# Two decoder layers on one core: the order of part three set anew, with the turning steps and value products as streams of their own, and GpSimd's divisions in halves

## The reference

```
x = ln(x + attn(x))          # causal, 16 heads of 64, bias on q, k, v
x = ln(x + xattn(x, ctx))    # 16 heads of 64, 64 keys, no mask
x = ln(x + ffn(x))           # an attention over nested widths 128, 64, 32, 16: 8 heads of 16
```

## Time and profile before

| | |
|---|---|
| median of three runs | 1757.98 us |
| the profiled execution | 1755.88 us, of which the span from first to last instruction is 1753.8 us |
| PE busy | 1543.1 us (88%), 14032 instructions |
| DVE busy | 1148.2 us (65%) |
| ACT busy | 958.4 us (55%) |
| POOL busy | 485.2 us (28%) |
| mean granted TensorE clock | 0.968 |

### The profile page before, as it was taken

The page is one execution under the profiler, slowest core; times in us unless marked ns, Lnnn a source line. Parts: engine busy times, 40 slices in busy tenths (PEclk is TensorE's granted clock), DMA queues, the critical chain, the costliest instruction groups (busy, mean ns, idle before and its releaser), DMA issues.

```text
span 1753.8 us, 35652 instructions
## 1 busy us (share of the span) xinstructions
PE 1543.1 (88%) x14032; PEld 1005.1 (57%) x14048; DVE 1148.2 (65%) x2246; ACT 958.4 (55%) x2412; POOL 485.2 (28%) x527
## 2 busy tenths in 40 slices
PE   5898889988868978999999999999999999999874
PEld 2555555555536855655656656655656656655642
DVE  5287777787754443676776776776775776775662
ACT  1655566556532225656656656656656656656532
POOL 1001110111006623333323333333323323333310
PEclk9999999999978889999999999999999999999996
DMA  8521111211129550010011010010010010000000
GB/s 262 210 74 61 50 47 65 66 47 44 54 88 145 106 171 4 22 43 31 25 43 31 25 43 31 25 43 31 25 43 31 25 43 31 7 25 28 4 4 4
DMA packets 64551, 94.68 MB, mean 54 GB/s; under 512 B 9250, under 2 KB 46995, under 8 KB 63652
## 3 DMA queue, kind: packets, MB, share of 16 engines
q1 hardware_dynamic: 61059, 88.54, 15.2%
q0 software_dynamic: 2560, 3.46, 2.2%
q10 hardware_dynamic: 768, 0.40, 0.1%
HBM read 55.37 MB, written 38.80 MB: 54 GB/s over the span
## 4 chain that ended last, share of the span: by engine, by line
PE 62%; DVE 23%; ACT 7%; issue 5%; POOL 2%; DMA 1%; ACTq 0%; DVEq 0%; POOLq 0%; PEld 0%; PEldq 0%
PE psum L710 6%; PE psum L856 5%; PE psum L785 4%; PE psum L650 4%; PE psum L930 4%; PE psum L923 3%; PE psum L675 3%; PE psum L833 3%; PE psum L882 2%; DVE negative_peak L1219 2%; PE psum L721 2%; PE psum L790 2%; PE psum L717 2%; PE psum L665 2%; DVE kx L1337 2%
## 5 line engine op out<-in xcount | busy, mean ns | idle before, releaser
L1219 DVE TENSOR_REDUCE negative_peak<-psum 128x4 f32<-128x1024 f32 x128 | 155.7, 1217 | 130.2 <-PE psum L717 121.3
L1095 ACT ACTIVATE prob<-psum 128x768 f32<-128x768 f32 (+1 forms) x192 | 158.8, 879 | 101.8 <-PE psum L816 61.3
L1391 POOL TENSOR_TENSOR rstd<-moments,eps 128x2 f32<-128x2 f32 x64 | 15.5, 242 | 627.7 <-DVE moments L1141 627.7
L1075 ACT ACTIVATE prob<-psum,negative_peak 128x256 f32<-128x256 f32 x256 | 117.9, 473 | 101.4 <-DVE negative_peak L1219 101.4
L1401 POOL TENSOR_TENSOR prob<-prob,row_sum 128x1024 f32<-128x1024 f32 x64 | 121.2, 1894 | 152.5 <-DVE row_sum L1200 152.5
L710 PE MATMUL psum<-kt,qt 64*128 64x256 f32 x1024 | 145.8, 403 | 3.6 <-ACT prob L1075 1.6
L856 PE MATMUL psum<-prob,v_big 128*64 128x256 f32 x1024 | 139.9, 394 | 6.8 <-ACT prob L1089 6.0
L1237 DVE TENSOR_REDUCE kt<-psum 128x4 bf16<-128x1024 f32 (+2 forms) x112 | 132.1, 1215 | 10.4 <-PE psum L742 10.4
L710 PEld LDWEIGHTS psum<-kt,qt 64*128 64x128 f32 x1024 | 89.8, 187 | 39.7 <-issue 28.4
L856 PEld LDWEIGHTS psum<-prob,v_big 128*64 128x64 f32 x1024 | 62.7, 137 | 72.1 <-issue 29.7
L1075 ACT ACTIVATE qb<-psum,negative_peak 128x256 f32<-128x256 f32 x128 | 59.0, 472 | 65.3 <-DVE negative_peak L1219 65.3
(11 more groups left out here) (315 smaller groups left out, 3614.2 us busy)
## 6 DMA issues: line engine op xcount, KB each, us to landing
zd<-kx SPq DMA_DIRECT2D x24, 512.0 KB, 6.2
union<-zd SPq DMA_DIRECT2D x16, 768.0 KB, 4.2
w_late<-ad SPq DMA_DIRECT2D x16, 512.0 KB, 3.7
w_late<-vd SPq DMA_DIRECT2D x16, 512.0 KB, 4.7
ad<-union SPq DMA_DIRECT2D x16, 256.0 KB, 2.2
vd<-union SPq DMA_DIRECT2D x16, 256.0 KB, 2.3
xg<-union SPq DMA_DIRECT2D x16, 192.0 KB, 2.0
w_late<-in_w1T SPq DMA_DIRECT2D x1, 2816.0 KB, 9.6
```

The source lines that it names most:

```text
L1075: last = nc.scalar.activation(rows[:, o:o + 256], banks[:, u, 256 * n:256 * n + 256], ACT.Exp, bias=negative_peak[s][:, c, u, n:n + 1], ac ...
L1095: nc.scalar.activation(prob_of[a][s][:, slot + 2 * i:slot + 2 * i + 2, 0:n], v.pair(step, i)[:, :, 0:n], ACT.Exp, scale=a.scale).then_inc( ...
L1219: nc.vector.tensor_reduce(negative_peak[s][:, which, :, :], banks.rearrange("p u (n k) -> p u n k", n=2), axis=AX.X, op=ALU.max, negate=Tr ...
```

## The change

Three things change. `pair_steps` now makes plain streams: the main streams keep S and E of pairs 6, 7, 0, 1, 2, 3, while the eight T steps of each sequence become streams G (s0) and H (s1), and the eight P steps streams I and J. TURNS3 and AHEAD3 are new: ten streams, set in another order. And GpSimd's division of 128x1024 weights is issued as two instructions of 128x512, the second of which raises the semaphore.

```diff
-def pair_steps(s):
+def pair_steps(kinds, s, first=0):
 
-    st = lambda kind, *n: [(kind, L1, s, PAIR_ORDER[i]) for i in n]
-    out = st("S", 2) + st("E", 2) + st("T", 0) + st("S", 3) + st("E", 3) + st("P", 0)
-    for i in range(4, len(PAIR_ORDER)):
-        out += st("T", i - 3) + st("S", i) + st("E", i) + st("P", i - 3)
-    return out + st("T", 5) + st("P", 5) + st("T", 6) + st("P", 6) + st("T", 7) + st("P", 7)
+    return [(kind, L1, s, c) for c in PAIR_ORDER[first:] for kind in kinds]
...
-    main = lambda s: ([("Q", L1, s, 0), ("Q", L1, s, 1)] + pair_steps(s)
+    main = lambda s: ([("Q", L1, s, 0), ("Q", L1, s, 1)] + pair_steps("SE", s, 2)
...
-    return [main(s) for s in AB] + [front(s) for s in AB] + [values(s) for s in AB]
+    return ([main(s) for s in AB] + [front(s) for s in AB] + [values(s) for s in AB] + [pair_steps("T", s) for s in AB]
+            + [pair_steps("P", s) for s in AB])
...
-TURNS3 = ("D B D B2 F2 C B2 A D B C A B4 C A B A B D C B A C2 A B4 A2 B C B4 A B3 E B C A B A C A B A B A4 B C "
-          "B A B A E B A D E D B A C B A2 D C A B2 D A C D C D A B2 A4 E B A D B A2 B A4 B A3 B A B A2 D A B A "
-          "F B A4 B2 A3 D B2 A2 B F B A2 B A B2 D B A2 B2 A B")
-AHEAD1, AHEAD3 = (22, 17, 6, 0, 0, 0, 0), (33, 0, 14, 10, 4, 2)
+TURNS3 = ("D B C B A B F D C B2 C F A D B F B C A J B J H A2 C H C J2 A B H B A2 B C B H A B E J2 A B A H C2 A2 "
+          "H C E A J2 A2 C A2 B3 A C D A E B A D B D C B A2 D A B D G A D A B G A3 B A2 E B2 A D A2 B C A2 I B "
+          "I G B A2 F B G A D B A I2 B G A B G B2 I2 B G D B G B I B I B2 D B D A2 B H B A B H")
+AHEAD1, AHEAD3 = (22, 17, 6, 0, 0, 0, 0), (17, 0, 14, 11, 4, 1, 8, 2, 8, 0)
...
-                rows = rows_l1[s][PAIR_ORDER.index(c) % 4].rearrange("p (n k) -> p n k", n=4)
-                by = row_sum[s][:, c, :, :].rearrange("p u n -> p (u n)").unsqueeze(2).to_broadcast([128, 4, T])
-                nc.gpsimd.tensor_tensor(rows, rows, by, ALU.mult).then_inc(y.rows_ready[s], 1)
+                for u in range(2):
+                    rows = rows_l1[s][PAIR_ORDER.index(c) % 4][:, 512 * u:512 * u + 512].rearrange("p (n k) -> p n k", n=2)
+                    by = row_sum[s][:, c, u, :].unsqueeze(2).to_broadcast([128, 2, T])
+                    last = nc.gpsimd.tensor_tensor(rows, rows, by, ALU.mult)
+                last.then_inc(y.rows_ready[s], 1)
```

More of the change, by code:

```diff
@@ L153, in interleaved @@
     for turn in turns.split():
-        k = "ABCDEFG".index(turn[0])
+        k = "ABCDEFGHIJ".index(turn[0])
         for _ in range(int(turn[1:] or 1)):
```

## The result

The changed kernel takes **1677.22 us** (median of four runs, 1672.35 to 1685.17) against 1761.39 for the kernel before on the same chip (1751.51 to 1766.0): a ratio of the means of 0.9534, 95% interval 0.9475 to 0.9592.

What follows compares the result with a forecast made beforehand. PE was taken to bound part three, so only its idle time could be won: 24.9 us in seven bodies, 2.5 filling, 1.0 last body, together 28.4 off 1755.9; 1729 us predicted, range 1707 to 1757.

Steps and rivals of the forecast that it cites:

- The waits: PE's idle time in a full body of part three: from 7.56 to 4.0 us, 24.9 won in seven bodies.
- XT of L1F s0: PE's step awaiting x_norm in the s0 chain: 4.4 us of work ahead, x_norm ready at 4.0, its 1.8 wait gone.
- XT to Q: In the s0 chain, the time between these PE steps: 1.8 us before, 2.3 with T and K between.
- XT of s1: In the s1 chain, PE's step awaiting x_norm, ready at 5.4 us against 5.4 of work: a wait of 0 to 0.3.
- The 4.3 of XT of L1 s0: PE's waits in ring M for the copy of a pair of P steps, 4.3 us in seven bodies: would go.
- what such a sum can't see: Many short PE waits at a dozen places in a body: 2.7 us before, 2.8 allowed after.
- The halves: GpSimd divisions cut in two, about 1.05 us each: gain taken as 0, cost 0 to 0.2 us a body.
- The filling: While part three's pipeline fills, P waits 3.2 us for ACT's copies of T: 2.5 of it won.
- the last body: Emptying ends on s1's cross and nested attention, a chain no order shortens: 1 us won, for its s0 half.
- All of it comes off: Rival for PE's waits: the short ones go too, 51 us won, 1707; chance 0.13.
- Into other waits: Rival: ACT and DVE run full in bursts, waits return as rings not emptied: 1746 to 1763; chance 0.26.
- slower: Rival: ACT's 1.6 us idle ahead of exponentials stays with each burst S step, 38 us lost, 1796; chance 0.11.

Runs made afterwards that it cites:

- run 10: Kernel before with the two divisions after the s0 norm, all divisions in halves, and P steps of L1 in pairs, order otherwise old: 1740.69 us.
- run 11: Changed kernel with S s1 6 moved next to S s1 7 and E s1 6 one place behind: 1667.91 us, ratio 0.9522 to the kernel before.
- run 4: Kernel before, whole divisions, with the first P step of each pair moved next to the second: 1774.2 us, ratio 1.0114.
- run 7: Changed kernel with seven further moves that put steps of one tile shape side by side: 1710.76 us, ratio 0.9767 to the kernel before.
- run 6: Changed kernel with the two divisions put back ahead of the s0 norm, and divisions whole: 1702.63 us (one run).
- run 1: Changed kernel with each division whole again, order as changed: 1677.05 us, ratio 0.957 to the kernel before.
- run 2: Kernel before with divisions in halves, old order kept: 1733.25 us, ratio 0.9886.
- run 3: Changed kernel with the pairs of P steps split by one or two steps each: 1697.97 us, ratio 0.9692 to the kernel before.
- run 8: Changed kernel once more, unaltered, measured beside the kernel with seven further moves: 1669.61 us, ratio 0.9525 to the kernel before.
- run 9: Kernel before with E s1 3 and E s0 4, and so their undivided divisions, after the s0 norm: 1739.53 us (one run).
- run 5: Changed kernel with the two divisions put back ahead of the s0 norm, still in halves: 1680.01 us (one run).

## Why the prediction was wrong

**The step that failed** is the sentence "PE bounds this part, its clock is full, and the change neither adds nor removes a matmul. So the new order can win only what PE idles". The first half holds: 6468 matmuls on either side. The second doesn't follow. What PE spends on the same matmuls depends on which stands behind which, and on how often PE waits; the order took 36.2 out of PE's own time in seven bodies, where the sum had 0 and the page after was to show "still about 867". By the second count that is 2.0 a body for changes of shape, 2.7 for the hand-overs behind waits that are gone, and 0.5 for the clock. The rows that I quoted couldn't show it, as each P of the earlier trace rows stands alone between steps of other shapes; the trace of before could: there a T starts 0.32 behind the last matmuls of a P, which among themselves follow at 0.22. I read start-to-start costs per step and took them as fixed, and a wait as costing its idle time and no more.

The Trainium skill, "TensorEngine Tiling (Array Packing)", section "Key Properties", says that changing the tiling mode, as against using another tile of it, drains TensorE. It gives no price. The spacings agree that a change costs time, 0.16 us; runs 10 and 11, which take out 13 and 2 changes and hardly touch the number of waits, come to 0.18 and 0.16 each.

**The waits** were forecast at 4.0 a body and are 2.98 (20.9 in seven). Without the halves they are 3.93. That this meets the forecast is in part luck, since only 1.2 of the 4.0 were named and the rest was an allowance; but the steps that placed the work were right. XT of L1F s0 had 4.4 of work ahead of it and x_norm was to be ready at 4.0; counted from the end of W, 864.80, XT begins 4.28 later and x_norm ends 3.9 later. XT to Q was 2.3, and is 2.04. XT of s1 was to wait 0 to 0.3, and waits 0.3. The 4.3 of XT of L1 s0 are gone. Of the 2.8 allowed for "what such a sum can't see", 1.0 is what halves would have taken away; 0.7 is a wait at a V of L1, which I hadn't found, and T s0 1 waits 0.6, not 0.1 to 0.2.

**The halves** were the second miss: taken at 0, "from 0 to 0.85 a pair", and worth 1.06 a body in the new order, 2.03 in the old. The pair's bound was wrong (3.33 to 1.62 is 1.7), and most of the gain in the new order, 0.7, came from one instruction, the mask product of L1F, which was on PE's path and in none of my sums. The Trainium skill, "SBUF — State Buffer", section "SBUF: two separate sides", has the shared port pair locked for a whole instruction; VectorE's rows here agree, and begin to move when a division or a half ends. What was wrong is what I drew from it, that halves give pairs nothing; each of the two waits for an end that comes sooner.

**The filling** brought 4.4 for 2.5 predicted, **the last body** 9.4 for 1.0. In the last, waits are 5.0 fewer (40.1 to 35.0 with the end's transfers) and own time 4.4, with 44 changes of shape instead of 53. I had called it a chain that no order shortens. The 9 changes would be 1.4 of the 4.4 at 0.16 each (an estimate); the rest, with a clock that is low in much of this stretch, I did not separate.

Against the sum: 68.3 for 24.9, 4.4 for 2.5, 9.4 for 1.0, and -2.0 ahead of part three; 51.7 more than forecast: 36.2 of own time and 7.2 of waits (the halves) in the seven bodies, 8.4 in the last, 1.9 in the filling, less 2.0.

**The rivals.** "All of it comes off", 1707, assumed 1.2 of waits a body (2.98 in truth) and the same fixed own time; no case had PE getting faster. "Into other waits" and "slower" did not come: PE's waits at T are 0.6 a body though ACT idles as before ahead of the exponentials, since PE has other work there. Runs 4 and 7 show that these rivals were no phantoms: the same kind of move in another place of the list made 4 to 4.5 us of waits a body.

## What to carry to other kernels

Where TensorE is the bound, count in the trace how often consecutive matmuls change tile shape and how often TensorE waits, and price both from start-to-start spacings: an engine that is busy all the time can be spending a part of it, here 18 of 123 us, on the order of its work, and a wait that goes can give back more than its idle time. A move that saves such changes pays only if the moved step was not the cover of a wait, so look at who waits behind its old place before setting steps side by side. And cut a long GpSimd instruction in two wherever a short VectorE instruction on TensorE's path can meet it; the price here was 0.2 us of an idle engine.

## What the runs showed of the hardware

**The granted clock falls after some waits, and the work behind pays.** In two of the seven full bodies before, own time is 1.63 longer. The view of stretches shows one place, behind an XT that had waited 1.77 for x_norm and a Q that had waited 0.49 (stretch, busy times, clock in the third column from the end):

```profile
887.40:890.90 3.50, 3.44 (x12) 1.94 (x12) 0.46 (x1) 1.97 (x6) 0.34 (x1) 0.53 0.00 0
```

0.53 is about the lower of the clock's two levels, 1.2 of 2.4 GHz. In the next body the same waits were followed by a clock of 1.00. With whole early divisions (run 6) XT waits 2.7, and the clock falls in every second body; PE's timeline in one of these:

```profile
994.11 0.69 PE L643 MATMUL psum<-ident,x_norm 128*128 128x128 f32 x2 [2.71 <-DVE x_norm L1158]
994.59 1.92 PE L794 MATMUL psum<-ident,prob 128*128 128x128 f32 x8
...
998.54 1.04 PE L794 MATMUL psum<-ident,prob 128*128 128x128 f32 x8
```

The same eight transposes take 1.92 just behind the wait and 1.04 four microseconds later. No full body dips in the runs where no wait of PE exceeds 1.1 us (after, runs 1, 2, 3, 8, 9 and 11), nor in runs 5 and 7, where the longest are 1.9 and 1.7; but in run 10 one dip stands behind waits of 0.86 and 0.64. A wait can so cost more than its length; what decides in which body it does stayed open.

**A change of tile shape costs TensorE 0.10 us at the change, into a full 128\*128 tile as out of it, and 0.06 in the mean in the spacing behind it** (tables above). **A wait costs about 0.22 us more than the idle time that the view of waits shows**, 4.7 us for 21 waits in a body before and 2.0 for 9 after.
